# Weights' scale multiplications on GpSimd, and one reciprocal for two units, in a two-layer attention and FFN kernel

## What is computed

```
def fp4_quant_dequant(x):                    # blocks of 16
    scale = max(max|xb| / 6, 1e-12)
    xn = xb / scale
    idx = searchsorted(_MID, |xn|)
    return _GRID[idx] * sign(xn) * scale
# first attention, per head
scores = scores - max(scores); attn = softmax(scores)
attn = clip(attn, 1e-12); attn = attn / sum(attn); ctx = attn @ Vh
```

## Time and profile before

| | us |
|---|---|
| median of 3 runs | 961.46 (960.75 to 961.52) |
| the profiled execution, its own time | 961.48 |
| its span, first to last instruction | 959.6 |
| opening's heads | about 30 to 101 |
| first, second, third crossing's heads | about 264 to 333, 493 to 562, 722 to 791 |

### The profile page before, as it was taken

How to read it: one execution, slowest core, us unless ns; L and a number is a source line. 1 busy time by engine, 2 the same in 40 slices (tenths; PEclk the granted TensorE clock), 3 DMA queues, 4 the chain that set the end, 5 groups by cost and what they waited for, 6 DMA issues and landing times.

```text
span 959.6 us, 15982 instructions
## 1 busy us (share of the span) xinstructions
PE 902.0 (94%) x5514; PEld 587.4 (61%) x5514; DVE 674.2 (70%) x2153; ACT 615.8 (64%) x1681; POOL 198.3 (21%) x312
## 2 busy tenths in 40 slices
PE   6889999999999999999999999999999999999986
PEld 2555565767555565577665656567756556657744
DVE  4999882763889785474588879266488988647348
ACT  3788435972879643794578943498287964369544
POOL 3200001762000000475000000177300000047300
PEclk9999999999999999999999999999999999999999
DMA  9500100000000000000000010000000000000000
GB/s 296 192 1 2 28 0 23 2 1 1 1 1 24 3 26 23 1 2 1 0 1 13 12 28 1 23 1 2 1 0 2 17 8 1 0 1 2 1 1 22
DMA packets 14558, 18.32 MB, mean 19 GB/s; under 512 B 3088, under 2 KB 11664, under 8 KB 14480
## 3 DMA queue, kind: packets, MB, share of 16 engines
q1 hardware_dynamic: 12288, 15.40, 4.8%
q10 hardware_dynamic: 2064, 1.91, 0.7%
q0 software_dynamic: 128, 0.01, 0.0%
HBM read 15.21 MB, written 2.10 MB: 18 GB/s over the span
## 4 chain that ended last, share of the span: by engine, by line
PE 61%; DVE 22%; ACT 11%; issue 4%; POOL 1%; POOLq 0%; DVEq 0%
PE bank L1082 24%; PE bank L1097 9%; PE bank L1278 6%; PE bank L1258 5%; PE bank L1352 5%; PE bank L1194 4%; ACT ring L593 4%; DVE row_max L884 4%; PE bank L1171 2%; ACT ring L634 1%; PE bank L1210 1%; PE bank L1137 1%; ACT ring L517 1%; DVE ring L892 1%; PE bank L1324 1%
## 5 line engine op out<-in xcount | busy, mean ns | idle before, releaser
L435 POOL TENSOR_TENSOR rstd<-var_eps,minus_half 128x2 f32<-128x2 f32 x32 | 23.4, 735 | 589.2 <-DVE var_eps L798 589.2
L517 ACT ACTIVATE ring<-bank 128x512 f32<-128x512 f32 x224 | 123.4, 610 | 19.2 <-PE bank L1097 19.1
L446 POOL TENSOR_TENSOR ring<-ring,row_inv 128x256 f32<-128x256 f32 x192 | 112.1, 613 | 101.9 <-DVE row_inv L979 101.9
L1097 PE MATMUL bank<-ident_s,ring 128*128 128x128 f32 x768 | 105.3, 279 | 5.3 <-POOL ring L446 2.3
L1097 PEld LDWEIGHTS bank<-ident_s,ring 128*128 128x128 f32 x768 | 82.6, 141 | 40.2 <-issue 17.4
L634 ACT ACTIVATE ring<-ring,row_max 128x256 f32<-128x256 f32 x192 | 95.1, 497 | 17.3 <-DVE row_max L972 17.3
L593 ACT ACTIVATE ring<-bank,row_max 128x256 f32<-128x256 f32 x192 | 88.2, 492 | 4.7 <-DVE row_max L884 4.7
L972 DVE CUSTOM_DVE_ANT_0 ring<-bank,maskbias 128x256 f32<-128x256 f32 x192 | 70.7, 420 | 23.4 <-issue 23.4
L884 DVE TENSOR_REDUCE row_max<-bank 128x2 f32<-128x512 f32 x128 | 79.4, 683 | 5.9 <-PE bank L1171 5.1
L1082 PE MATMUL bank<-wgu_s,act_s 128*128 128x352 f32 x256 | 78.4, 459 | 0.0
L1082 PE MATMUL bank<-ctxT_s,wk_s 128*128 128x512 f32 x160 | 75.6, 596 | 0.7 <-DVE v L870 0.7
(11 more groups left out here) (163 smaller groups left out, 1661.3 us busy)
## 6 DMA issues: line engine op xcount, KB each, us to landing
x_s<-x SPq DMA_DIRECT2D x4, 512.0 KB, 3.9
ctxT_s<-ctxT SPq DMA_DIRECT2D x4, 512.0 KB, 3.6
w_s<-w SPq DMA_DIRECT2D x2, 1024.0 KB, 16.4
out<-act_s SPq DMA_DIRECT2D x16, 128.0 KB, 1.7
wk_s<-wk SPq DMA_DIRECT2D x1, 1024.0 KB, 13.5
wv_s<-wv SPq DMA_DIRECT2D x1, 1024.0 KB, 14.8
wq_s<-wq SPq DMA_DIRECT2D x1, 1024.0 KB, 16.4
wo_s<-wo SPq DMA_DIRECT2D x1, 1024.0 KB, 16.6
```

The lines of the kernel that those rows point to most:

```text
L446: ins = pool.tensor_tensor(probs1[i % PRING1][:, a, :], probs1[i % PRING1][:, a, :], row_inv[:, i, a:a + 1].to_broadcast([P, SEQ]), ALU.mult)
L517: act.activation(probsT[u % TRING][:, :, :].rearrange("p a q -> p (a q)"), psum(at, key)[:], ACT.Copy).then_inc(drain(at, key), 1)
L1097: ins = pe.transpose(psum(at, key)[:, c * SEQ + a * P:c * SEQ + (a + 1) * P], tile[:, a, c * P:(c + 1) * P], ident_s[:])
```

## The change

It does two things.

First, the multiplication by the scale (L770) of pieces 1 to 4 is no longer VectorE's third instruction of `round_piece`, but is issued by GpSimd (`multiply_piece`), which waits until VectorE's second step is done. VectorE goes on to the next round's row maxima. `scale_piece(n)` now waits until the piece before has been multiplied, since it overwrites `scale`. GpSimd's `mask_to_bias` comes behind the first such multiplication and waits for the first maximum of round 2 in place of that of round 1.

Second, in all four groups, `normalize` of one unit becomes `normalize_two`: it waits for the exponentials of two units, takes one reciprocal of 128 x 4 sums, waits for it once, and then scales both units with four instructions.

```diff
+POOL_PIECES = range(1, 5)
@@ gpsimd
+            def multiply_piece(n):
+                nb = weight_pieces[n].shape[-1] // BLOCK
+                blocks = weight_pieces[n].rearrange("p (b e) -> p b e", b=nb)
+                pool.wait_ge(wrounded, ROUND_OPS * n + 2)
+                pool.tensor_tensor(blocks, blocks, scale[:, 0:nb].unsqueeze(2).to_broadcast([P, nb, BLOCK]), ALU.mult).then_inc(wrounded, 1)
...
-            pool.wait_ge(mask_loaded, 16)
-            pool.wait_ge(max0, 5)
-            mask_to_bias()
+            for n in POOL_PIECES:
+                if n == 2:
+                    pool.wait_ge(mask_loaded, 16)
+                    pool.wait_ge(max0, 9)
+                    mask_to_bias()
+                multiply_piece(n)
@@ vector, quantize_round
-                dve.wait_ge(signal, done + 2)
-                dve.tensor_tensor(blocks_of(val, nb), ..., ALU.mult).then_inc(signal, 1)
+                if multiplied:
+                    dve.wait_ge(signal, done + 2)
+                    dve.tensor_tensor(blocks_of(val, nb), ..., ALU.mult).then_inc(signal, 1)
@@ scale_piece
+                if n >= 1:
+                    dve.wait_ge(wrounded, ROUND_OPS * n)
@@ layer0_heads
-                def normalize(u):
-                    dve.wait_ge(*is_drained(at, ("s0", u)))
-                    dve.reciprocal(row_inv[:, u, :], row_sum[:, u, :]).then_inc(inv0, 1)
-                    dve.wait_ge(inv0, units + u + 1)
-                    for a in range(2):
-                        ins = dve.tensor_scalar(probs0[u % PRING0][:, a, :], ..., ALU.mult, ALU.max)
-                    ins.then_inc(clipped0, 1)
+                def normalize_two(first):
+                    both = range(first, first + 2)
+                    for u in both:
+                        dve.wait_ge(*is_drained(at, ("s0", u)))
+                    dve.reciprocal(row_inv[:, first:first + 2, :], row_sum[:, first:first + 2, :]).then_inc(inv0, 1)
+                    dve.wait_ge(inv0, (units + first) // 2 + 1)
+                    for u in both:
+                        for a in range(2):
+                            ins = dve.tensor_scalar(probs0[u % PRING0][:, a, :], ..., ALU.mult, ALU.max)
+                        ins.then_inc(clipped0, 1)
...
-                    for i in round_units0(r):
-                        if i == 2 and g is not None:
-                            output_bias(at)
-                        normalize(i)
+                    normalize_two(4 * r)
+                    if r == 0 and g is not None:
+                        output_bias(at)
+                    normalize_two(4 * r + 2)
```

More of the change, by code:

```diff
@@ L757, in quantize_scale, with quantize_round @@
                                          ALU.mult, ALU.mult).then_inc(signal, 1)
-            def quantize_round(val, size, sized, signal, k):
+            def quantize_round(val, size, sized, signal, k, multiplied=True):
                 n, done = val.shape[-1], ROUND_OPS * k
@@ L768, in quantize_round @@
                 dve.scalar_tensor_tensor(val, size, LEAST_STEPS, val, ALU.max, ALU.subtract, reverse1=True).then_inc(signal, 1)
-                dve.wait_ge(signal, done + 2)
-                dve.tensor_tensor(blocks_of(val, nb), blocks_of(val, nb), sc.unsqueeze(2).to_broadcast([P, nb, BLOCK]), ALU.mult).then_inc(signal, 1)
+                if multiplied:
+                    dve.wait_ge(signal, done + 2)
+                    dve.tensor_tensor(blocks_of(val, nb), blocks_of(val, nb), sc.unsqueeze(2).to_broadcast([P, nb, BLOCK]), ALU.mult).then_inc(signal, 1)
             def quantize(src, k, between=None):
@@ L782, in scale_piece @@
                     dve.wait_ge(rows_loaded, 16 * 5)
+                if n >= 1:
+                    dve.wait_ge(wrounded, ROUND_OPS * n)
                 quantize_scale(weight_pieces[n], wscaled, n)
             def round_piece(n):
-                quantize_round(weight_pieces[n], piece_temps[n % 2][:, 0:weight_pieces[n].shape[-1]], wsteps, wrounded, n)
+                quantize_round(weight_pieces[n], piece_temps[n % 2][:, 0:weight_pieces[n].shape[-1]], wsteps, wrounded, n, n not in POOL_PIECES)
             def ln_tile(n, t, src):
@@ L885, in row_maxima @@
                                       negate=True).then_inc(max0, 1)
-                def normalize(u):
-                    dve.wait_ge(*is_drained(at, ("s0", u)))
-                    dve.reciprocal(row_inv[:, u, :], row_sum[:, u, :]).then_inc(inv0, 1)
-                    dve.wait_ge(inv0, units + u + 1)
-                    for a in range(2):
-                        ins = dve.tensor_scalar(probs0[u % PRING0][:, a, :], probs0[u % PRING0][:, a, :], row_inv[:, u, a:a + 1], CLIP,
-                                                ALU.mult, ALU.max)
-                    ins.then_inc(clipped0, 1)
+                def normalize_two(first):
[6 more added lines that the diff above has]
+                        for a in range(2):
+                            ins = dve.tensor_scalar(probs0[u % PRING0][:, a, :], probs0[u % PRING0][:, a, :], row_inv[:, u, a:a + 1], CLIP,
+                                                    ALU.mult, ALU.max)
+                        ins.then_inc(clipped0, 1)
                 for r in range(ROUNDS0):
```

## The result

The changed kernel takes 965.21 us (median of 6 runs, 962.52 to 965.76) against 961.49: ratio 1.0036, with a 95% interval of 1.0023 to 1.0049. It is slower, by more than what I took for the limit of a measurement (0.2%), and by 3.7 us where I had forecast 1.3. The most likely time, 962.8, and "the same" were not what came; the direction was. Put on the scale of the kernel before (961.46 times 1.0036) the change stands at 964.9: inside the wide range of 960.0 to 965.0, but outside the forecast's own, 961.9 to 963.3.

The account below looks back on a forecast made before the run. The prediction took VectorE's work after an even round's last exponential to bound the kernel. Opening -1.9 and three crossings +3.2 made +1.3 us: 962.8 from 961.48, own range 961.9 to 963.3, wide range 960.0 to 965.0.

Parts of the forecast that it names:

- the wide range of 960.0 to 965.0: Whole kernel: the prediction's wider range in us, beside the forecast's own 961.9 to 963.3, which had chance 0.55.
- What bounds the kernel: Crossings and opening: VectorE's work after an even round's last exponential stands in the chain; less VectorE work mostly gains nothing.
- the loop through bank 6: Crossings, every two rounds: exponentials, fourth unit's scalings, finished tile, four maxima, `over_sums`, then TensorE's products, whose bank `over_sums` frees.
- The pair's 0.53 us per loop: Crossings, rounds 2 and 4: last exponential to next maximum 0.53 us longer; 1.06 per crossing, +3.2 for three.
- The second wait at zero: Reciprocals waiting for two semaphores: 0 to 0.20 us at some ten places, 0 to 2.0 in all; taken as zero.
- the first rival: At the pairs' reciprocals: waits for two add up, 0.06 us per place passing 0.2%; 963.4 to 965 us, chance 0.23.
- the margin of 0.52: Crossings, after round 6: VectorE idle 0.52 us until the scores came, taken to swallow the pair's 0.53.
- The transposes of units 0 and 1, ready in time: Crossings, TensorE: transposes need the pair's scalings some 1.1 us after its reciprocal and find them ready, at no cost.
- The opening, 1.9 us earlier: Opening: round 7 starts 2.0 us earlier, 0.15 goes back; piece 5, layer norm and output product start 1.9 earlier.
- The stall by the mask: Opening, round 2: `mask_to_bias` ends at 46.4 and holds up the first pair, which has until 47.3.
- GpSimd's multiplications at zero: Opening: 768 columns take 1.8 us on GpSimd beside VectorE's maxima and cost nothing; bound 6.5 us if all in VectorE's way.

Follow-up runs that it names:

- e1: Kernel before with only GpSimd's multiplications of pieces 1 to 4, each unit keeping its own reciprocal: 958.37 us against 961.68, ratio 0.9967.
- e2: Kernel before with only the reciprocals of two units (`normalize_two`), nothing moved to GpSimd: 968.19 us, ratio 1.0064.
- e3: The change, but only units 0 and 1 of a round share a reciprocal; units 2 and 3 have one each: 959.87 us, ratio 0.9988.
- e7: Kernel before, with the reciprocals of units 1 and 3 also waiting for the unit before them, a semaphore long fired: 963.58 us, ratio 1.002.
- e6: The change plus three unused products of zeros on TensorE in its idle time at 21 to 24 us: 965.83 us, ratio 1.0038.
- e4: The change, but `mask_to_bias` starts ahead of round 2's maxima, not behind the first of them: 964.4 us, ratio 1.0031.
- e8: e5 with `mask_to_bias` started ahead of round 2's maxima, as in e4: 957.43 us against 961.59, ratio 0.9957.
- e5: e1 plus three unused products of zeros on TensorE in its idle time at 21 to 24 us: 957.92 us, ratio 0.9963.
- e9: e8 with piece 5 also multiplied on GpSimd, from a scale tile of its own: 959.03 us, ratio 0.9969.

## Why the prediction came out as it did

- **What bounds the kernel**: right. Less work on VectorE didn't count; the loop through bank 6 did, at the places named.
- **The pair's 0.53 us per loop**: right mechanism, shown by e1 (13.67 without pairs), e2 (14.29 with nothing else) and e3. Its size is off. A loop takes 0.60 longer (14.28 against 13.68), and a crossing 1.3 us and not 1.06, three 4.0 and not 3.2. The 0.07 is the second wait (e7).
- **The second wait at zero**: this is the step of the sum that failed. I had bounded it by 0 and 0.20 and chosen zero, since the earlier unit has fired 0.9 us before. The runs show 0.06 to 0.07 each time that it is tight. It counts in two loops of each crossing and in the opening's loops. After round 6 it counts for nothing: round 7's maxima start 1.17 us behind their scores (317.02 and 318.19), as before (1.16), so the pair's 0.53 and the wait are swallowed there. That is against the first rival, which had the margin of 0.52 used up.
- **The transposes of units 0 and 1, ready in time**: wrong, by a little. They take 1.16 and not 1.09, and between the first two products of a crossing (6.77, was 6.71) and behind round 6 (13.70 from 307.36 to 321.06, was 13.63) that shows. e2 and e3 have the same, e7, without pairs, hasn't; so it goes with the pair of units 0 and 1. So a crossing is 1.06 for the scalings, 0.14 for the second wait in two loops and 0.13 for these transposes: 1.33, and 1.3 was measured. e3's crossing, 0.60 longer than before (229.54 and 228.94), is made up likewise: 0.23 twice and 0.13. The first rival gave 963.4 to 965; without the clock the change comes to 964.0 (below), but not for that rival's reason alone.
- **The opening, 1.9 us earlier**: 1.46 in an execution without a fall of the clock (e6). Counted from the first scores, round 1 starts 1.37 earlier, as forecast, round 3 1.3, not 1.45, and round 7 1.8, not 2.0; most of that is the second wait at three places. Round 7 then gives back 0.47 and not 0.15. From its first exponential to the end of the scalings it takes 5.34 in e6 (82.97 to 88.31), where I had 5.06: the reciprocal starts 0.29 behind the last exponential, not 0.20, and its first scaling 0.40 behind it, not 0.20. The profiles of the change and of e4 have the same pause there, e2's hasn't; what it waits for is open. The stall by the mask, which I had taken as hidden, was hidden (e4 against e6). Only with one reciprocal for each unit does it show (e8 against e5). Against e5's opening of 73.20, which has GpSimd's multiplications without pairs, the pairs cost 1.98 in the opening too.
- **GpSimd's multiplications at zero**: right. They take 1.50 for 768 columns (I had 1.8), and the maxima beside them 2.48 as without. e9 shows the other side of it: beside scalings from SBUF to SBUF the same operation costs more than it saves, 1.80 in place of 0.73 for two. The Trainium skill (SBUF — State Buffer, "Who interferes with whom") says that a VectorE instruction with at most one SBUF input does not contend with GpSimd outside the two-port modes, and that one in a two-port mode does. The maxima agree with it. The scalings agree if they run in a two-port mode, which no row names; their speed fits it, since within SBUF a TENSOR_SCALAR of 512 columns takes 0.43 us (L849 of the kernel before) and a TENSOR_TENSOR of 512 takes 0.69 (L834).
- **The clock**: not in the sum, and the largest of the terms that were missed. With -1.5 and +4.0 the change would be 2.5 us slower, 964.0 from the profiled 961.48. The profiled 965.76 has some 1.7 more. The fall at 24 us costs 1.69, the earlier start that came with it gives 0.76 back; the fall at 48 us brings the other 0.8 (77.67 - 75.18 - 1.69). The kernel before had no such fall in the opening of its profile, and its runs lie within 1.2 us; the change has spans at three levels. e5 and e6 show that the fall at 24 us doesn't come when TensorE's idle time before it is filled. It is **not** shown that the change causes the falls: the length of the warm-up, which the change doesn't touch, differs from kernel to kernel (5.52 to 6.77), and all profiles with the 1.84 us idle and a warm-up under 6 us have the fall at 24 us (the change, e1, e2, e3, e7), while the two over 6.4 don't (the kernel before, e4). What sets that time stays open, and so does what brings the falls at 48 and 99 us.

## What to carry to other kernels

Work that is merged to save an instruction should not be placed behind the last arrival of a loop: what is saved was idle time, and what is added stands in the chain. Move work to GpSimd under maxima of VectorE that read PSUM, where it cost nothing here, and not beside scalings within SBUF, where it cost more than it saved. And count every wait that an instruction gets, also one that has fired.

## What the hardware showed that I had not expected

- A second semaphore wait on a VectorE instruction costs 0.06 to 0.07 us, even when it has fired 0.9 us before (e7: 0.27 against 0.20, and 13.75 against 13.68 for a loop).
- TensorE's granted clock fell to half for some 3 us after idle times of 1.84 to 2.04 us in the opening, at 24, 48 or 96 to 99 us (e9, e3, e6), in some kernels and not in others with the same idle time or more (2.20 us in e2, at 89.92, with no fall). In the gap before 24 us three products of zeros left no fall there in four profiles (e5, e6, e8, e9), and e5's five runs lie within 0.9 us.
- GpSimd's multiplication of 128x768 by a broadcast 128x48 took 1.50 us, less in proportion than its addition of 128x1024 in 2.35 to 2.37.
